# A copy moved ahead of squares on ScalarE, and a norm's close moved later on VectorE, in a fused RWKV and MoE block

## The reference

```python
h = layernorm(x) * (1 + ca) + sa                 # "first norm"
# RWKV block on h:
a  = layer_norm(h, ln1_g, ln1_b)                 # "next norm", kind 1 in the kernel
k, v, r = mix(a, mk) @ Wk.T, mix(a, mv) @ Wv.T, mix(a, mr) @ Wr.T    # time mix
x2 = h + (sigmoid(r) * wkv(k, v)) @ Wo.T
c  = layer_norm(x2, ln2_g, ln2_b)                # kind 2 in the kernel
kk = mix(c, ck) @ Wkey.T; kv = silu(kk) @ Wval.T # channel mix
sr = sigmoid(mix(c, cr) @ Wcr.T)
x4 = x2 + sr * kv
```

## Time and profile before

| what | value |
|---|---|
| runs, us | 927.0, 929.03, 1271.75 |
| median, us | 929.03 |
| profiled execution, us | 921.43 |
| its span, first to last instruction, us | 919.7 |
| mean granted TensorE clock | 0.990 of full |
| TensorE busy | 887.2 us, 96% of the span |
| VectorE, ScalarE, GpSimd busy | 502.7, 402.0, 384.2 us |

### The profile page before, as it was taken

How to read it: one execution, slowest core, us unless ns; L and a number is a source line. 1 busy time by engine, 2 the same in 40 slices (tenths; PEclk the granted TensorE clock), 3 DMA queues, 4 the chain that set the end, 5 groups by cost and what they waited for, 6 DMA issues and landing times.

```text
span 919.7 us, 13596 instructions
## 1 busy us (share of the span) xinstructions
PE 887.2 (96%) x4264; PEld 715.2 (78%) x4265; DVE 502.7 (55%) x967; ACT 402.0 (44%) x688; POOL 384.2 (42%) x282
## 2 busy tenths in 40 slices
PE   6899989999998999999999999999999999999996
PEld 2367778788776888888888888888887887888875
DVE  4685999884847111454135513651496444444388
ACT  3575875875645432322232223225444333333352
POOL 3231120100022546226202530258537699998473
PEclk9899999999999999999999999999999999999998
DMA  9659577654155328396214321466435788775787
GB/s 357 218 176 307 167 244 253 204 185 135 49 189 201 114 92 274 119 288 212 92 34 158 118 92 35 154 218 212 161 115 195 244 255 264 271 272 207 250 248 192
DMA packets 122401, 174.07 MB, mean 189 GB/s; under 512 B 8792, under 2 KB 70232, under 8 KB 119280
## 3 DMA queue, kind: packets, MB, share of 16 engines
q1 hardware_dynamic: 59472, 111.58, 35.5%
q0 software_dynamic: 9216, 34.61, 12.1%
q10 hardware_dynamic: 53664, 27.26, 10.3%
HBM read 97.60 MB, written 75.83 MB: 189 GB/s over the span
## 4 chain that ended last, share of the span: by engine, by line
PE 84%; ACT 5%; DMA 4%; DVE 3%; issue 2%; POOL 1%; SPq 0%; ACTq 0%; DVEq 0%
PE kk_ps L427 6%; PE kv_ps L427 6%; PE kk_ps L429 6%; PE kv_ps L429 6%; PE kk_ps L428 6%; PE kv_ps L428 6%; PE mm_ps L427 6%; PE mm_ps L428 6%; PE mm_ps L429 6%; PE up_ps L427 4%; PE dn_ps L427 3%; PE dn_ps L429 3%; PE dn_ps L428 3%; PE up_ps L428 3%; PE up_ps L429 3%
## 5 line engine op out<-in xcount | busy, mean ns | idle before, releaser
L1576 DVE TENSOR_TENSOR silu<-kk_ps,silu 128x512 fp32r<-128x512 f32 x64 | 44.3, 691 | 199.9 <-ACT silu L2266 199.6
L2262 ACT ACTIVATE kk_ps<-kk_ps 128x512 f32<-128x512 f32 x64 | 37.2, 582 | 206.8 <-PE kk_ps L429 206.8
L427 PE MATMUL kk_ps<-xk,cm_w 128*128 128x512 f32 x256 | 100.9, 394 | 0.0
L427 PE MATMUL kv_ps<-cm_w,silu 128*128 128x512 f32 x256 | 100.5, 393 | 0.0
L429 PE MATMUL kk_ps<-xk,cm_w 128*128 128x512 f32 x256 | 99.8, 390 | 0.0
L429 PE MATMUL kv_ps<-cm_w,silu 128*128 128x512 f32 x256 | 99.7, 390 | 0.0
L428 PE MATMUL kk_ps<-xk,cm_w 128*128 128x512 f32 x256 | 99.6, 389 | 0.0
L428 PE MATMUL kv_ps<-cm_w,silu 128*128 128x512 f32 x256 | 99.6, 389 | 0.0
L2439 POOL TENSOR_TENSOR rs<-mv,neghalf 128x4 f32<-128x4 f32 (+2 forms) x13 | 15.8, 1217 | 152.6 <-DVE mv L1327 139.9
L2432 POOL TENSOR_TENSOR cm_w<-stage,cm_w 128x1024 fp32r<-128x1024 f32 x16 | 38.7, 2422 | 91.1 <-ACT cm_w L2026 72.3
L2490 POOL TENSOR_TENSOR rs<-mv,neghalf 128x1 f32<-128x1 f32 x16 | 16.1, 1008 | 127.4 <-DVE mv L1601 127.4
(11 more groups left out here) (306 smaller groups left out, 2345.9 us busy)
## 6 DMA issues: line engine op xcount, KB each, us to landing
xs_s<-zero ACTq DMA_DIRECT2D x13, 1024.0 KB, 7.9
ys_s<-zero ACTq DMA_DIRECT2D x13, 1024.0 KB, 6.3
xsb<-xs_s SPq DMA_DIRECT2D x44, 256.0 KB, 3.7
ys_s<-ysb SPq DMA_DIRECT2D x41, 256.0 KB, 4.1
ex_raw<-in_wex POOLq DMA_DIRECT2D x9, 1024.0 KB, 6.7
stage<-in_wcm SPq DMA_DIRECT2D x16, 512.0 KB, 3.7
wmod<-in_wmod SPq DMA_DIRECT2D x6, 1024.0 KB, 11.7
ex_raw<-in_wex SPq DMA_DIRECT2D x6, 1024.0 KB, 7.2
```

Of the source, the lines that this page charges most:

```text
L427: pe.matmul(out, lhs[0], rhs[0], start=first, stop=False)
L1576: dve.tensor_tensor(silu[:, g % NSILU, 1, :], kk_ps[g % 2][:, :], silu[:, g % NSILU, 0, :].bitcast(F32), ALU.subtract).then_inc(s_silo, 1)
L2262: act.activation(kk_ps[g % 2][:, :], kk_ps[g % 2][:, :], ACT.Silu).then_inc(s_silu, 1)
```

## The change

In batches 1 and 2, where a batch is still to come, steps move on ScalarE and VectorE; in batch 3, which has no next norm, only ScalarE's copies move, and batch 0 is as it was. No instruction is added or removed.

On ScalarE, `to_hT(2, b - 1, [0, 1])` goes from behind the R mixes and `exps(b, [2])` to directly behind the first of the four squares. The second square goes behind `exps(b, [3])`, the third and fourth behind `to_hT(2, b - 1, [2, 3])`. On VectorE, `variance(1, b + 1)` goes from behind `wkv(b, 0)` to behind the first two S mixes, and `centred(1, b + 1)` from behind the third R low half to behind the second S low half.

```diff
--- before.py
+++ after.py
@@ -1473,13 +1473,13 @@
                 v_out(b, 0)
                 mixed_lo("R", b, 1)
                 wkv(b, 0)
-                if more:
-                    variance(1, b + 1)
+                if more and b == 0:
+                    variance(1, 1)
                 mixed("R", b, 3)
                 v_out(b, 1)
                 mixed_lo("R", b, 2)
-                if more:
-                    centred(1, b + 1)
+                if more and b == 0:
+                    centred(1, 1)
                 wkv(b, 1)
                 mixed_lo("R", b, 3)
                 if b:
@@ -1490,12 +1490,16 @@
                     differences(2, b - 1, [2, 3])
                     mixed("S", b - 1, 0)
                     mixed("S", b - 1, 1)
+                    if more:
+                        variance(1, b + 1)
                 v_out(b, 3)
                 wkv(b, 3)
                 if b:
                     mixed_lo("S", b - 1, 0)
                     mixed("S", b - 1, 2)
                     mixed_lo("S", b - 1, 1)
+                    if more:
+                        centred(1, b + 1)
                     mixed("X", b - 1, 0)
                     mixed("S", b - 1, 3)
                     mixed_lo("S", b - 1, 2)
@@ -2166,7 +2170,9 @@
                     clear_slots(6 * b + 0)
                 mixed_hi("R", b, [0, 1])
                 if more:
-                    squares(1, b + 1)
+                    squares(1, b + 1, [0] if b else range(TT))
+                if b:
+                    to_hT(2, b - 1, [0, 1])
                 if b == 0:
                     rows_out(3, tp_ps[0][:, :, :].rearrange("p j c -> p (j c)"))
                 mixed_hi("R", b, [2])
@@ -2174,17 +2180,19 @@
                 mixed_hi("R", b, [3])
                 if more:
                     clear_slots(6 * b + 1)
-                if b:
-                    to_hT(2, b - 1, [0, 1])
                 exps(b, [3])
                 if more:
                     clear_slots(6 * b + 2)
+                if b and more:
+                    squares(1, b + 1, [1])
                 if b == 0:
                     rows_out(4, tp_ps[1][:, :, :].rearrange("p j c -> p (j c)"))
                     weight_hi(6)
                     weight_hi(7)
                 if b:
                     to_hT(2, b - 1, [2, 3])
+                    if more:
+                        squares(1, b + 1, [2, 3])
                     mixed_hi("S", b - 1, [0, 1])
                 if more:
                     hn_out(1, b + 1, [0, 1])
```

## The result

| | us |
|---|---|
| before, median of 13 runs | 927.94 |
| changed, median of 13 runs | 932.48 (929.83 to 936.69) |
| ratio, changed to before | 1.0054, 95% interval 1.0042 to 1.0066 |
| profiled execution of the changed kernel: span | 933.2 |
| its mean granted clock | 0.981 |

The change makes the kernel slower by 0.54%, about 5.0 us. That is inside 2%, and the interval does not contain 1, so the slowdown is clear of the noise. One of the 13 runs before took 1271.75 us and is left out of the ratio.

A forecast was written before the change was run, and what follows sets the result against it. TensorE, busy 887.2 of 919.7 us, bounds the kernel, so only its waits or slow clock can be won. Batch 1 +3.1, batch 2 -0.55, batch 3 +0.3 sum to +2.9 on 929.03: about 932 us, range 925 to 938.

The forecast's parts named there:

- signs of being wrong: In batch 1 `nm` at 0.16 us or TensorE's wait under 4 us, or a batch 2 turn wait over 1.5 us.
- The copies end the wait at the turn: TensorE's transposes behind V block 2 no longer wait for `hT` in batches 1 to 3; longest wait 3.40 us.
- The next norm closes late: Batch 1: variance at 123.85, `hn` complete at 136.4, TensorE waiting 6.8 us from 129.6.
- The weight halves hold VectorE: Batch 1: third S mix stands from 126.1 to 127.9 and `nm` from 129.1 to 131.0 beside GpSimd's S weight halves.
- the third rival: Batch 1: third S mix slips ahead of the first weight half, saving 1.8 us; sum about +1.1, 930 us; chance 0.16.
- DMA issues "I cost that at nothing": Two slot-clearing DMA issues on ScalarE's queue stay behind the same R mixes, start under 2 us later, cost nothing.
- The slow clock, 1.5 us: Batch 1: slow matmuls behind the new wait for `hn` cost 1.5 us, as behind the old wait; bounds 0 to 3.
- Batch 2, -0.55 us: Batch 2: TensorE arrives 1.15 us earlier but waits 0.6 for `hn`; net -0.55 us, between -1.15 and 0.
- Batch 3, +0.3 us: Batch 3: the 1.0 us won is taken back at O block 0, waiting for S's sigmoid; +0.3, between -0.1 and +1.
- Later stages only shift: Stages after this one are bound by TensorE and only shift in time, adding no term.

The follow-up runs named there:

- VectorE's part alone: Kernel before with only VectorE's moves (variance and centred late), ScalarE in the old order; ratio 1.0022.
- batch 3 in old order: Changed kernel with ScalarE's old order in batch 3 alone; ratio to the kernel before 1.0050.
- copies alone: Kernel before with ScalarE's two copies behind the first square, the other three squares following, VectorE in the old order; ratio 1.0005.
- third clear later: Changed kernel with the third clear DMA of batch 1 issued behind the first two S mixes; ratio to the kernel before 1.0037.
- before with weight halves early: Kernel before with the S weight halves split in batch 0 by ScalarE (high) and GpSimd (low); ratio 0.9984.
- before with S low halves zero: Kernel before with GpSimd writing zeros as the low half of the S weights; ratio 1.0001.
- changed with weight halves early: Changed kernel with the S weight halves split in batch 0 by ScalarE (high) and GpSimd (low); ratio to the kernel before 0.9966.
- copies alone with weight halves early: Kernel before with ScalarE's copies behind the first square, VectorE's order old, S weight halves split in batch 0; ratio 0.9950.
- changed with S low halves zero: Changed kernel with GpSimd writing zeros as the low half of the S weights; ratio to the kernel before 1.0006.

## Why the prediction was right, and where it was off

The time of 932.48 us lies in the range, 0.5 from the 932 given. That it is so near is luck: the kernel before came out at 927.94 and not 929.03, and the effect was 5.0 us and not 2.9. The direction, the wait for `hn` and its cause were as forecast, none of the signs of being wrong came, and the 2.1 us missing are in the sizes of terms. The forecast 2.9 lies outside the interval of the ratio. Step by step:

- *The copies end the wait at the turn.* Right in every batch: TensorE turned at 115.06 (forecast 115.1), full clock from 114 to 123.
- *The next norm closes late.* Right, and shown by the trace of VectorE's part alone. The variance was forecast at 123.85 and came at 125.56; with the third clear moved it came at 123.78, so VectorE's own chain was right. The wait of 7.74 us is over the 6 to 7 forecast.
- *The weight halves hold VectorE.* Right: the third S mix 2.08 us, `nm` 1.70. Writing zeros took 0.48% off the changed kernel. GpSimd's first half began at 126.77, one us ahead of the third S mix; the third rival, where that mix slips ahead, did not happen. The rule of the Trainium skill (SBUF — State Buffer, "Who interferes with whom"), that the second to issue blocks, fits each of these meetings with a weight half. The zeros agree with its other clause, that a GpSimd instruction that only writes does not contend: while they were written, the third S mix took 0.76 us in the changed kernel and `nm` 0.15 in the kernel before.
- *DMA issues "I cost that at nothing".* This step was wrong. The prediction had the issues start later than before; the third started 2.16 us earlier, close behind the second, and took 2.35 us, with the copies of the second turn behind it. Moving it gave back 1.7 us of the turn's start. The turn was only 1.1 us later than forecast (137.47 to 136.4), because the steps from the variance to the last `hn` took 0.6 us less than forecast, `rsqrt` 1.01 for 1.47 among them; two errors partly cancel.
- *The slow clock, 1.5 us.* It was 2.5, inside the bounds of 0 to 3, and with the DMA issue the other half of the miss. The prediction took it from the one wait seen, with twice that as its bound. The runs show that the length of a wait doesn't give it: 2.9 us behind a wait of 6.05, 2.05 behind one of 7.80 (batch 3 in old order), none behind 2.66.
- *Batch 2, -0.55 us.* It was -0.14. At the next norm's turn it was -0.23, since `hn` was complete some 0.3 us later than forecast; the last 0.1 is lost at steps I did not follow.
- *Batch 3, +0.3 us.* To the start of O block 0 it was +0.12. The 1.6 us of slow matmuls behind a wait of 1.79 us were not foreseen; they are in two of the six traces with that wait.
- *Later stages only shift.* By the ratios, yes: 5.0 us in all against the 5.2 by which O block 0 is late. The profiled execution alone would have said 13.5; why it does is open.

The sum of the terms as measured in the trace, 5.19 - 0.14 + 0.12 = 5.2 us, is near what the ratio gives. Part of that is luck too, as the 2.5 us of slow clock in it were 2.05 in the execution with a wait of 7.80; the 1.6 us behind it are in the profiled execution and are not in every run.

## What to carry to other kernels

A wait on the bounding engine is worth what the next-latest engine leaves of it: removing 5 us of wait and slow clock by the copies alone gave nothing that can be told, since VectorE, held by the weight halves, was nearly as late behind the same wait. When the close of a chain is moved later, list everything on the other engines' queues that moves with it, here the weight halves behind `rsqrt`, and look what they then stand beside. List as well what starts earlier because a stall has left, here the third clear. Taking the disturbing work out of the stretch, as with those halves (1.0054 to 0.9966), did more than any order of the steps around it.

## What the runs showed of the hardware

- The third DMA issue of batch 1 on ScalarE's queue took long where it stood close behind the clear issued before it, and ScalarE's compute stood meanwhile (1.82 us idle in the changed kernel). With 4.4 us or more between the two starts it took 0.54 to 0.55 us (before, copies alone, third clear later); with 3.0 us 1.17, 1.65 and 1.85 (before with weight halves early, VectorE's part alone, before with S low halves zero); with 2.5 us 1.71, 2.35, 2.38, 2.45 and 2.53 (changed with weight halves early, changed, batch 3 in old order, copies alone with weight halves early, changed with S low halves zero). The long issues all ended 4.2 to 5.0 us after the start of the one before. No run tells whether it was the bytes in flight or something else that held them.
- GpSimd's zeroing of two 128x1024 tiles took 1.85 us and held up no VectorE step with two SBUF inputs (the third S mix, 0.76 us); the two subtractions of the same size took 5.27 and held up two (2.08 and 1.70 us).
- What a wait of TensorE does to the granted clock behind it could not be told from its length. The same wait of 1.79 or 1.80 us ahead of O block 0 was followed by 0.60 and 0.74 in the next 2 us (changed, third clear later) and by full clock in four other traces (copies alone, changed with S low halves zero, both with early halves). The table has the waits for `hn` at the first turn of the next norm in batch 1, the granted clock of the 2 us from that turn on, and how much longer than the 3.64 us of the kernel before it was to the second turn.

| kernel | wait, us | granted clock | longer by, us |
|---|---|---|---|
| changed, batch 3 in old order | 7.80 | 0.50 | 2.05 |
| changed | 7.74 | 0.50 | 2.50 |
| changed, third clear later | 6.05 | 0.50 | 2.89 |
| changed, S low halves zero | 5.07 | 0.50 | 1.83 |
| changed, weight halves early | 2.66 | 1.00 | 0.03 |
| VectorE's part alone | 2.45 | 0.86, then 0.50 | 1.64 |
| copies alone | 2.22 | 0.50 | 1.63 |
| copies alone, weight halves early | 1.74 | 1.00 | 0.06 |
